# Self-attention: the rotation's sum ahead of the context's scaling, the transposes of rotated queries and keys ahead of those of the context

## The reference

```python
residual = hidden_states
x = rms_norm(hidden_states, ln_in_w)
mixed = jnp.where(vm, x @ v_qkv, x @ l_qkv)          # an expert for each token
q, k, v = jnp.split(mixed, 3, axis=-1)
q, k, v = (heads(q, NH, HD), heads(k, NH, HD), heads(v, NH, HD))   # NH = 16, HD = 16
q, k = apply_rotary(q, k, position_ids, l)           # q * cos + rotate_half(q) * sin
ctx = sdpa(q, k, v, causal=True)
ctx = ctx.transpose(0, 2, 1, 3).reshape(b, l, H)
attn_out = jnp.where(vm, ctx @ v_dense, ctx @ l_dense)
hidden_states = residual + attn_out
```

## Time and profile before

| | us |
|---|---|
| median of 3 runs | 2259.29 |
| the runs | 2249.55 to 2263.94 |
| the profiled execution | 2255.95 |
| its span, first to last instruction | 2254.1 |
| PE busy | 2092.3 (93%) |
| DVE busy | 1375.4 (61%) |
| ACT busy | 1142.4 (51%) |
| POOL busy | 813.3 (36%) |

### The profile page before, as it was taken

How to read it: one execution, slowest core, us unless ns; L and a number is a source line. 1 busy time by engine, 2 the same in 40 slices (tenths; PEclk the granted TensorE clock), 3 DMA queues, 4 the chain that set the end, 5 groups by cost and what they waited for, 6 DMA issues and landing times.

```text
span 2254.1 us, 63424 instructions
## 1 busy us (share of the span) xinstructions
PE 2092.3 (93%) x23904; PEld 1683.3 (75%) x23905; DVE 1375.4 (61%) x2831; ACT 1142.4 (51%) x2595; POOL 813.3 (36%) x1045
## 2 busy tenths in 40 slices
PE   7978999889979997999999979997999989979998
PEld 4646777655659997788888859986777756659997
DVE  6756888656753333666666655554888757763333
ACT  4765666455653332544544535354666546663332
POOL 1654444278632221111121112224444336642222
PEclk9989999989989998999999989998999989989999
DMA  7425444120131113100000010004444320011111
GB/s 230 122 82 161 134 136 129 52 86 23 29 106 58 57 61 101 37 2 2 2 2 3 2 39 19 26 22 130 137 132 136 110 77 28 28 44 61 56 58 35
DMA packets 105988, 155.08 MB, mean 69 GB/s; under 512 B 24100, under 2 KB 82289, under 8 KB 105617
## 3 DMA queue, kind: packets, MB, share of 16 engines
q1 hardware_dynamic: 87952, 95.39, 13.7%
q0 software_dynamic: 16560, 55.23, 7.6%
q10 hardware_dynamic: 1232, 1.05, 0.2%
HBM read 86.69 MB, written 56.28 MB: 63 GB/s over the span
## 4 chain that ended last, share of the span: by engine, by line
PE 80%; DVE 8%; issue 2%; ACT 2%; DMA 1%; another core or an unknown queue 1%; POOL 1%; POOLq 0%; DVEq 0%; ACTq 0%; SPq 0%
PE ps_all L2394 4%; PE ps_all L2396 4%; PE ps_all L2395 4%; PE ps_all L1626 3%; PE ps_all L1598 3%; PE ps_all L1189 3%; PE ps_all L1175 3%; PE ps_all L1207 3%; PE ps_all L1968 2%; PE ps_all L2419 2%; PE ps_all L2421 2%; PE ps_all L2420 2%; PE ps_all L2404 2%; PE ps_all L1612 2%; PE ps_all L1157 2%; PE ps_all L1642 2%
## 5 line engine op out<-in xcount | busy, mean ns | idle before, releaser
L403 POOL TENSOR_TENSOR a_probs<-a_probs,a_sm 128x1024 f32<-128x1024 f32 x32 | 60.9, 1903 | 345.5 <-DVE a_sm L398 345.5
L1370 POOL TENSOR_TENSOR pool_w<-s_qkt,const 128x512 f32<-128x512 f32 x128 | 131.5, 1049 | 88.8 <-ACT s_qkt L1304 88.8
L2394 PE MATMUL ps_all<-f_wh,f_xh 128*128 x396 | 154.0, 389 | 5.3 <-DVE f_xl L2540 5.3
L1748 POOL TENSOR_TENSOR c_kx<-c_qkt,const 128x512 f32<-128x512 f32 x128 | 130.9, 1042 | 76.2 <-ACT c_qkt L1691 75.7
L2396 PE MATMUL ps_all<-f_wl,f_xh 128*128 x396 | 148.4, 375 | 0.0
L2395 PE MATMUL ps_all<-f_wh,f_xl 128*128 x396 | 148.4, 375 | 0.0
L2100 ACT ACTIVATE self_w<-ps_all,a_q_bias 128x256 f32<-128x256 f32 x128 | 53.8, 471 | 183.4 <-PE ps_all L1944 183.4
L2535 DVE SCALAR_TENSOR_TENSOR f_h<-ps_all,rstd,f_act_g 128x688 f32<-128x688 f32 x66 | 61.7, 934 | 135.2 <-PE ps_all L2396 135.2
L374 DVE TENSOR_REDUCE s_mx<-ps_all 128x8 f32<-128x512 f32 x128 | 82.5, 687 | 75.7 <-PE ps_all L1175 75.7
L2458 ACT ACTIVATE f_act_g<-ps_all,rstd 128x688 f32<-128x688 f32 x66 | 55.2, 837 | 134.9 <-PE ps_all L2396 134.9
L1699 ACT ACTIVATE c_pt<-ps_all 128x512 f32<-128x512 f32 x128 | 69.5, 594 | 104.6 <-PE ps_all L1612 95.1
(11 more groups left out here) (339 smaller groups left out, 6874.5 us busy)
## 6 DMA issues: line engine op xcount, KB each, us to landing
qkv_sorted<-pool_w SPq DMA_DIRECT2D x66, 392.0 KB, 2.4
pool_w<-pool_w SPq DMA_DIRECT2D x128, 68.0 KB, 2.2
s_x_in<-x_sorted SPq DMA_DIRECT2D x66, 128.0 KB, 2.3
f_x_in<-x_sorted SPq DMA_DIRECT2D x66, 128.0 KB, 2.0
x_res<-x_sorted SPq DMA_DIRECT2D x66, 128.0 KB, 2.2
x_sorted<-x_res POOLq DMA_DIRECT2D x1, 4224.0 KB, 17.6
l_rows<-in_x SPq DMA_DIRECT2D x32, 128.0 KB, 2.3
x_res<-in_x SPq DMA_DIRECT2D x32, 128.0 KB, 3.1
```

The costliest lines, as they stand in the source:

```text
L1370: ins = nc.gpsimd.tensor_tensor(kx[:, p % 2, c], qkt[:, p % 2, 2 + c].rearrange("p (b k) -> p b k", b=2).unsqueeze(2) .broadcast_to([P, 2, ...
L1748: ins = nc.gpsimd.tensor_tensor(kx[:, p % 2, b], qkt[:, p % 2, 1, b * S:b * S + S].unsqueeze(1).broadcast_to([P, RH, S]), const[:, C_H8X:C ...
L2394: nc.tensor.matmul(bank, x_high, wh[:, w_at], start=(c == 0), stop=False)
```

## The change

Three places in the step loop of `self_attention` are put in another order; no function is changed.

```diff
@@ PE
+                        if has(p + 2):
+                            qk_t(p + 2)
                         if has(p - 1):
                             out_t(p - 1)
-                        if has(p + 2):
-                            qk_t(p + 2)
@@ ACT
+                        if has(p + 2):
+                            qkt_copy(p + 2)
                         if has(p - 1):
                             out_high(p - 1)
-                        if has(p + 2):
-                            qkt_copy(p + 2)
@@ DVE
                         if has(p + 2):
                             rope_products(p + 2)
+                            rope_sum(p + 2)
                         if has(p - 1):
                             out_norm(p - 1)
-                        if has(p + 2):
-                            rope_sum(p + 2)
```

## The result

Over 10 runs the changed kernel takes 2238.59 us (2227.81 to 2248.76), the kernel before 2257.67 us in its 10 runs (2249.55 to 2263.94). The ratio is 0.9926, with a 95% interval of 0.9908 to 0.9943: some 17 us (the medians differ by 19). That is less than the 1% which the prediction held to be the least that a measurement can tell, but ten runs of each kernel tell it clearly. The span of the profiled executions went from 2254.1 to 2236.5 us, by 17.6.

What follows compares the result with a forecast made beforehand. PE was taken to bound the kernel, with its wait for the rotation's sum removable: 8.6 us in full steps plus 0.3 per layer, 17.8 us over two layers, giving 2238.2 to 2241.5, named 2240 us; range 2231 to 2252.

Steps and rivals of the forecast that it cites:

- The bound: Full self-attention steps: PE limits, and idles 0.38 us each at L1157, waiting for the rotation's sum L1437 on DVE.
- The sum on DVE: Sum placed behind the products starts 0.45 us after L1432, exposing a 0.12 us wait; reciprocal 0.60 later, scaling 0.29 after that.
- The transposes on PE: L1157's four transposes go ahead of the context's two; L1167 comes 0.30 to 0.36 us sooner, middle 0.33, step 7.87 us.
- the margin of 0.07 us: At L1214 on PE: the context's scaled input is there at 289.53, its transposes are due at 289.60.
- the rival of the moved wait: PE waits at L1214 instead; reciprocal, scaling and signal each 0.1 late lose 0.23 of 0.33 us, 2251 us; chance 0.09.
- The copies on ACT: L1304 goes ahead of L1319, which follows 0.49 (near end) to 0.60 us later; L374's 1 us slack shrinks to nearly nothing.
- the copy's new place sets the step: Rival: L1319 follows after the whole 0.60, L374 starts at 291.35, step 7.97 us, 2244 us; chance 0.20.
- The rings: From the experiments: ways through PE, ACT and DVE back to their start, over the scaling (two steps) or sum (one step).
- Steps without a tile: Three steps per layer without projection, bound by DVE: L1167 0.10 us sooner each, 0.3 us a layer.
- The clock: Rival: PE's granted clock falls once more or less per stretch, 1.7 us each, 2231 to 2245 us; chance 0.10.
- slower: Rival: the way from maximum through PE, ACT and DVE to the next maximum, up to 7.97 us, exceeds 8.20; chance 0.06.
- The sum: Two layers of 26 full steps at 0.33 us and three at 0.10 give 17.8 us off the span.

Runs made afterwards that it cites:

- the two kernels that undo one half each: Against the kernel before: only DVE's order changed (sum ahead of reciprocal and scaling), ratio 1.0036; only PE's and ACT's order changed, ratio 1.0067.
- the delayed versions: The change with extra copies to unused tiles, ratios to the kernel before: one on ACT 0.9922, one on DVE 0.9957, two larger ones on ACT 0.9947.

## Why the prediction was right, point by point

**The bound.** PE, and its wait for the sum in the full steps: right. The wait is gone, and the two kernels that undo one half each show that it was this wait and that both halves are needed.

**The sum on DVE.** Right: L1437 starts 0.45 behind L1432, the reciprocal 0.61 behind that, the scaling 0.29 later. The exposed wait of 0.12 us is there too, 0.45 against 0.33 in all traces. It is the wait and not the form of the sum: in the kernel before, where the products were long done, the sum starts 0.34 behind the scaling (288.60 to 288.94). The Trainium skill, "VectorE: DVE Perf Modes", section "The DRAIN you can't avoid", found the semaphore free of charge in a chain of eight copies. These traces don't bear that out for this kernel.

**The transposes on PE.** The order is right, and so is the time at which the input is there (the scaling is seen 0.48 behind 284.63, at 285.11, for a matmul at 285.17). But the margin of 0.07 us was none. The weight load has to be 0.06 ahead of its matmul, so the input came just as it was needed, and a delay of 0.13 us on DVE cost the step 0.13. That the wait was not passed on is therefore partly luck: the rival of the moved wait was nearer than its 0.09 of chance says, and one of its three pieces late by 0.1 would, at the price of that delay, have cost 0.1 a step. The size was off by a little: 0.36 a step, the upper end of 0.30 to 0.36, where I took the middle and a step of 7.87. The mis-sized term is the last pair of transposes: I gave it part of the 0.05 us that only a pair behind a wait takes. Over the 50 steps behind step 1 that is 1.2 us; step 1 of each layer gave 0.09 instead of the 0.33 I counted, which takes 0.5 back.

**The copies on ACT.** The times are right (L1304 0.63 behind L1157, L1319 0.50 behind that, L1453 0.48 later), the slack before L374 is down to 0.11 us, nearly nothing as forecast, and the near end of 0.49 was the right one. Wrong was what follows from it. The rival "the copy's new place sets the step" took the time at which L374 could start for the step's bound, with 0.09 us of slack and 5.2 us for each 0.1 beyond. A later L374 is caught by further waits: a delay of 0.20 us on ACT cost nothing. The rings have 0.19 and 0.40 us of slack, and the price just past the first is by my sum half of that. The far end of my range for L1319, 0.11 us later, would have cost nothing. Its 0.20 of chance was too much, though it didn't shift the forecast.

**Steps without a tile.** 0.10 each forecast, 0.3 a layer; measured 0.3 a layer over steps 27 to 30. Single steps differ by more than that, because the lower clock falls on other steps: before it is steps 28 and 30 (9.53 and 7.62 us, clock 0.82 and 0.78), now 28, 29 and a part of 27 (9.14, 9.45 and 8.08 us, clock 0.84, 0.82 and 0.96). At a clock of 1.00 on both sides step 27 takes 7.93 us before and 7.84 now (second layer), 0.09 sooner, as forecast.

**The clock.** The rival gave up to 7 us either way. Between 405 and 438 us before, and 395 and 428 us now, the mean granted clock is 0.90 both times, so there it neither gave nor took. It shows in step 0 of the second layer, 1.06 us longer in this profile (and also in some of the others, in one layer or the other). In the first 2 us of that step the clock is 0.50 now and was 0.83 before, and the products of the scores, which everything in the step waits for, take 2.02 instead of 1.12 us. Over the whole step the mean is even a little higher now, 0.78 against 0.74: where the lower clock falls counts, not only how long it lasts.

**The moved wait, and slower.** At L1214 there is one wait of 0.2 us in 25 steps, though with no margin behind it. For a slower kernel one of the rings would have had to be longer than the old steps, 16.4 us for two and 8.20 for one; they are 15.49 and 7.44.

**The sum.** 17.8 us off the span was forecast, 17.6 are measured: 17.9 in the 52 full steps (forecast 17.2), 0.6 in those without a tile, and 0.9 given back, nearly all in that step 0. So the sum came out closer than its terms, which is luck, as is that the untouched stretch between the layers was equally long in both profiles.

## What to carry to other kernels

If an engine waits in the middle of its step for a producer that has been busy with something else, turn round both: the producer's order and the consumer's order are one change, and each alone made this kernel slower. Before pricing the next bound, walk every ring through the other engines until it closes, count over how many steps it does, and look for each wait on it: each is slack, and only their sum is the margin. Two rings can share most of their way and still have different slack and a different price. Count an input of a PE instruction as needed when its weight load starts, not when its matmul does. And look at the loop's last steps by themselves, where an engine that covers waits elsewhere has no work; an order of their own brought more per step there than the whole change, nearly half of it through PE's clock.

## What was not expected of the hardware

In these traces the weight load of a transpose starts 0.06 to 0.11 us ahead of its matmul when nothing is waited for, and at the same time as it behind a wait. Two transposes up to the mask take 0.32 us in the first case and 0.37 in the second, in the change, the delayed versions and the kernel before. Counted from the load of a pair that its input lets go, it is 0.37 to 0.38 in both. Two ACT copies of 128x512 that don't depend on each other start 0.49 to 0.50 apart although each lasts 0.60.
